# A fused six-part Macaron block on one NeuronCore: the last chunk's layer norm and choice of experts of the scan stage are made inside the second experts' stage

## The reference, cut to what matters

```python
x = L0_attn_x                                   # (8, 256, 256) float32
x = x + 0.5 * experts(layernorm(x))             # part 1, 16 experts, top 6, plus a shared one
x = x + selective_scan_block(layernorm(x))      # part 2, inner width 512, 16 states
x = x + 0.5 * experts(layernorm(x))             # part 3, the same weights as part 1
x = x + 0.5 * hadamard_ffn(layernorm(x))        # part 4
x = x + attention(layernorm(x))                 # part 5, 16 heads
x = x + 0.5 * hadamard_ffn(layernorm(x))        # part 6

def experts(x):
    scores = softmax(x @ gate_w.T)              # 16 experts
    w, ids = top_k(scores, 6); w = w / w.sum()
    c = combine(w, ids)                         # (token, expert) weights, 0 if not chosen
    out = sum_e c[:, e] * ((silu(x @ w1_e.T) * (x @ w3_e.T)) @ w2_e.T)
    return out + shared(x)
```

## Time and profile before

| | us |
|---|---|
| runs of the kernel | 2080.87, 2075.30, 2070.96 |
| median | 2075.3 |
| profiled execution, its time | 2073.7 |
| profiled execution, its span | 2071.9 |
| mean granted TensorE clock | 0.955 |

### The profile page before, as it was taken

The page is one execution under the profiler, slowest core; times in us unless marked ns, Lnnn a source line. Parts: engine busy times, 40 slices in busy tenths (PEclk is TensorE's granted clock), DMA queues, the critical chain, the costliest instruction groups (busy, mean ns, idle before and its releaser), DMA issues.

```text
span 2071.9 us, 26257 instructions
## 1 busy us (share of the span) xinstructions
PE 1865.6 (90%) x9448; PEld 1413.0 (68%) x9448; DVE 1353.3 (65%) x1828; ACT 933.4 (45%) x1769; POOL 570.6 (28%) x386
## 2 busy tenths in 40 slices
PE   5699999998779797898876999999999987999898
PEld 2488888887334353444434888888888875777787
DVE  4656656567099999989994565665676454666433
ACT  1223333333466577667552233332333326888322
POOL 1500000002177677677860000000000023555000
PEclk9899999999889999999997999999999988999999
DMA  4253223210022121122213232332221006653000
GB/s 175 88 155 103 77 86 103 62 62 26 21 66 76 57 66 62 56 66 62 69 53 92 85 104 62 100 95 71 62 74 50 1 8 140 113 115 73 31 21 21
DMA packets 86891, 150.86 MB, mean 73 GB/s; under 512 B 14376, under 2 KB 24232, under 8 KB 86248
## 3 DMA queue, kind: packets, MB, share of 16 engines
q1 hardware_dynamic: 86760, 149.17, 25.2%
HBM read 134.84 MB, written 14.29 MB: 72 GB/s over the span
## 4 chain that ended last, share of the span: by engine, by line
PE 72%; DVE 14%; issue 6%; ACT 5%; POOL 1%; SPq 1%; DMA 1%; DVEq 0%; ACTq 0%; POOLq 0%
PE psum L159 19%; PE psum L160 18%; PE psum L161 18%; DVE scan_state L1372 6%; PE psum L1225 4%; PE psum L1138 3%; PE psum L1165 1%; PE psum L1718 1%; DVE scan_state L1379 1%; PE psum L1146 1%; ACT attn_p L1850 1%; PE psum L1197 1%; PE psum L276 1%; PE psum L1697 1%; POOL scan_taps L1028 1%
## 5 line engine op out<-in xcount | busy, mean ns | idle before, releaser
L1041 POOL TENSOR_TENSOR scan_state<-scan_delta_u,scan_B_rows 128x1024 f32<-128x1024 f32 x128 | 301.8, 2367 | 171.5 <-PE psum L1225 124.0
L159 PE MATMUL psum<-xnT_hi,moe_w_hi 128*128 128x512 f32 x800 | 317.0, 396 | 4.6 <-DVE moe_w_lo L700 4.6
L160 PE MATMUL psum<-xnT_lo,moe_w_hi 128*128 128x512 f32 x800 | 315.5, 394 | 0.0
L161 PE MATMUL psum<-xnT_hi,moe_w_lo 128*128 128x512 f32 x800 | 312.9, 391 | 0.0
L1372 DVE TENSOR_TENSOR_SCAN scan_state<-psum,scan_state 128x1024 f32<-128x1024 f32 x128 | 292.2, 2283 | 3.1 <-POOL scan_state L1041 2.5
L768 DVE TENSOR_TENSOR moe_gated_up<-moe_gate_rows,psum 128x512 f32<-128x512 f32 x200 | 137.5, 688 | 239.2 <-PE psum L161 154.8
L410 POOL TENSOR_SCALAR rstd<-mean_var 128x2 f32<-128x2 f32 x48 | 10.7, 222 | 1020.0 <-DVE mean_var L444 1019.4
L724 ACT ACTIVATE moe_hidden<-psum 128x512 f32<-128x512 f32 x200 | 119.9, 600 | 377.4 <-PE psum L161 377.4
L1225 PE MATMUL psum<-scan_state,ident 128*128 128x512 f32 x512 | 255.8, 624 | 0.0
L159 PE MATMUL psum<-moe_w_hi,moe_hidden_hi 128*128 128x256 f32 x800 | 227.0, 284 | 9.1 <-DVE moe_hidden_lo L789 8.0
L161 PE MATMUL psum<-moe_w_hi,moe_hidden_lo 128*128 128x256 f32 x800 | 226.9, 284 | 0.0
(11 more groups left out here) (214 smaller groups left out, 3531.5 us busy)
## 6 DMA issues: line engine op xcount, KB each, us to landing
scan_B_rows<-scan_B SPq DMA_DIRECT2D x128, 256.0 KB, 3.1
moe_gate_rows<-gate_table SPq DMA_DIRECT2D x176, 128.0 KB, 2.9
moe_w_raw<-moe_pack SPq DMA_DIRECT2D x50, 384.0 KB, 3.8
attn_stack<-attn_rows SPq DMA_DIRECT2D x96, 128.0 KB, 5.4
moe_gate_rows<-gate_table SPq DMA_DIRECT2D x32, 224.0 KB, 3.0
ffn_w_raw<-ffn_pack SPq DMA_DIRECT2D x16, 384.0 KB, 3.7
moe_gate_rows<-gate_table SPq DMA_DIRECT2D x32, 160.0 KB, 2.7
moe_gate_rows<-gate_table SPq DMA_DIRECT2D x24, 192.0 KB, 2.9
```

Source lines behind the costliest of these rows:

```text
L159: e.matmul(out, wH, xH, start=start, stop=False)
L160: e.matmul(out, wH, xL, start=False, stop=False)
L161: return e.matmul(out, wL, xH, start=False, stop=stop)
L1041: e.tensor_tensor(self.st[q % self.NBUF][:], self.dtu[:, 2 * h:2 * h + 2, :], self.Bs[:, q % self.RING, :].unsqueeze(1).broadcast_to([P, 2 ...
```

## The change

For the experts' stage of part 3 a flag `guest` is set.

- `Tail.by_act` becomes a number: chunk 3 of the scan's tail normalises on DVE, with the shorter POOL sequence; chunks 0 to 2 stay on ACT.
- Jobs `g2` and `g3` of chunk 3 go from r = 23 and 25 to r = 4 and 5 (`LAST`). SP fetches the raw expert weights at r = 12 of chunk 3, ahead of that unit's B row, once g3's product is done. ACT splits the first tile at r = 24 (`lead_act`), DVE at r = 26 (`lead_dve`).
- PE runs gu(0) between the last y and out0. `tail.final` is left out on every engine.
- The tail of chunk 3 hangs behind steps 1 to 9 of the experts' stage: statistics at j = 1, 2, normalising at 2, 3, transposes at 2, 3, `xH` at 3, 4, `xL` at 4, `logits` at 5, `keep_logits` and `turn_logits` at 6, `choose` at 7, `turn_gates` at 8, `gates_hi` at 9. POOL runs its two steps from the experts' stage.
- SP stores the gates of chunks 0 to 2 right after the scan's last B row, waits for out1, fetches all five first gate rows, and stores chunk 3's gates at step 10, ahead of the gate rows of step 15.
- ACT waits for out1 before it splits the second tile.

```diff
-        if slot in (0, 2) and self.by_act:
+        if slot in (0, 2) and c < self.by_act:
...
-        if g == 0 and c == 0 and self.handed:
-            return self.before, NCH - 1, t
+        if (g == 0 and c == 0 and self.handed) or (self.guest and j < 10):
+            return self.before, NCH - 1, j
...
-    PE_SLOTS = {2: 1, 3: 3}
-    ACT_SLOTS = {3: 1, 4: 3}
+    PE_SLOTS = {2: 1, 3: 3, 5: 4, 6: 5, 8: 6}
+    ACT_SLOTS = {3: 1, 4: 3, 6: 4, 7: 5, 9: 6}
...
     def sync(self, e, meanwhile=None):
-        if self.prev:
+        if self.guest:
+            self.before.store_gates(e, self.gates[0], range(NCH - 1))
+            self.clear(e)
+            for j in range(self.PIECES):
+                self.piece(e, j)
+        elif self.prev:
             self.clear(e)
             self.first(e)
...
+                if self.guest and j + self.PIECES == self.G * (NCH - 1):
+                    self.before.store_gates(e, self.gates[0], (NCH - 1,))
...
+    def lead_pe(self, e):
+        self.gu(e, 0)
+
     def tensor(self, e):
-        self.gu(e, 0)
+        if not self.guest:
+            self.gu(e, 0)
...
     def lead_act(self, e):
-        self.prev.freed(e)
+        if self.guest:
+            self.prev.spent(e)
+        else:
+            self.prev.freed(e)
         self.split_hi(e, 0)
...
     def scalar(self, e):
         if not self.handed:
-            self.before.ready(e, NCH - 1)
+            if self.guest:
+                self.prev.freed(e)
+            else:
+                self.before.ready(e, NCH - 1)
...
+            if tt == 7 and self.guest:
+                tail.choose(e, tc, tail.bank())
...
+    LAST = {4: ("g2", 0), 5: ("g3", 0), 23: (None, 0), 25: (None, 0)}
...
+    def spent(self, e):
+
+        e.wait_ge(self.s_gin.sem, self.s_gin.at(4 * NCH))
+        e.wait_ge(self.s_Du.sem, self.s_Du.at(2 * NCH - 1))
+        e.wait_ge(self.s_dtu.sem, self.s_dtu.at(2 * NCH - 1))
...
     def sync(self, e):
         for q in range(self.N):
             c, h, n = self.unit(q)
+            if q == self.N - self.UNITS + 12 and self.next:
+                e.wait_ge(self.s_gin.sem, self.s_gin.at(4 * NCH))
+                self.next.first(e)
...
+        if self.next:
+            self.next.lead_pe(e)
         for name in ("out0", "out1"):
             job((name, NCH - 1), self.BANK)
-        self.tail.final(self.tail.pe, e)
+        if not self.next:
+            self.tail.final(self.tail.pe, e)
...
+            if q == self.N - 8 and self.next:
+                self.next.lead_act(e)
...
+            if q == self.N - 6 and self.next:
+                self.next.lead_dve(e)
```

More of the change, by code:

```diff
@@ L176, in __init__ @@
         self.home = None
-        self.by_act = False
+        self.by_act = 0
         self.back = back and not entry
@@ L386, in choose, with store_gates @@
         assert n[0] == self.r_v.per, n[0]
-    def store_gates(self, e, table):
-        for c in range(NCH):
+    def store_gates(self, e, table, chunks=range(NCH)):
+        for c in chunks:
             cols = slice(c * CHUNK, (c + 1) * CHUNK)
@@ L446, in norm @@
     def norm(self, e, c, p):
-        if self.last or self.by_act:
+        if self.last or c < self.by_act:
             return
@@ L500, in __init__ @@
         self.prev = self.next = None
-        self.handed, self.hands = handed, False
+        self.handed, self.hands, self.guest = handed, False, False
         tail.spare = True
@@ L595, in sync @@
     def sync(self, e, meanwhile=None):
-        if self.prev:
+        if self.guest:
[4 more added lines that the diff above has]
+        elif self.prev:
             self.clear(e)
             self.first(e)
-        if self.gates:
+        if self.gates and not self.guest:
             for j in range(2):
@@ L604, in sync @@
                 self.piece(e, j)
+        if self.gates:
             for j in range(self.N):
@@ L619, in pool @@
     def pool(self, e):
-        if self.handed:
+        if self.handed or self.guest:
             for slot in (0, 2):
@@ L673, in tensor @@
             tail, c, t = self.behind(j)
-            if t in self.PE_SLOTS:
+            if t in self.PE_SLOTS and (t < 5 or self.guest):
                 tail.pe(e, c, self.PE_SLOTS[t])
@@ L729, in scalar @@
             tail, c, t = self.behind(j)
-            if t in self.ACT_SLOTS:
+            if t in self.ACT_SLOTS and (t < 5 or self.guest):
                 tail.act(e, c, self.ACT_SLOTS[t])
@@ L916, in __init__ @@
         self.s_o = Sem(k, "o")
-        tail.by_act, tail.s_pw = True, Sem(k, "pw", 4, passes=NCH)
+        tail.by_act, tail.s_pw = NCH - 1, Sem(k, "pw", 4, passes=NCH)
         self.prior, used = {}, {}
@@ L983, in job @@
         name, ahead = self.JOBS.get(r, (None, 0))
+        if c == NCH - 1:
+            name, ahead = self.LAST.get(r, (name, ahead))
         return (name, c + ahead) if name and 0 <= c + ahead < NCH else None
@@ L1060, in pool @@
                 self.tail.pool(e, c - 1, 0 if r == 7 else 2)
-        for slot in (0, 2):
-            self.tail.pool(e, NCH - 1, slot)
+        if not self.next:
+            for slot in (0, 2):
+                self.tail.pool(e, NCH - 1, slot)
     def normed(self, e, c, i):
@@ L1357, in scalar @@
                 rows_hi(c + 1)
-        self.tail.final(self.tail.act, e, self.next and self.next.lead_act)
+            if q == self.N - 8 and self.next:
+                self.next.lead_act(e)
+        if not self.next:
+            self.tail.final(self.tail.act, e)
     def vector(self, e):
@@ L1428, in vector @@
             add(NCH - 1, p)
-        self.tail.final(self.tail.dve, e, self.next and self.next.lead_dve)
+        if not self.next:
+            self.tail.final(self.tail.dve, e)
 class Attention:
@@ L2111, in program @@
                                  (gates, ins["ones"]), tails[n - 1], tails[n]))
+                if n == 3:
+                    parts[-1].guest = tails[n - 1].spare = True
                 if n == 1:
```

5 lines of the change are left out of this document (3 added, 2 removed).

## The result

The changed kernel took 2063.7 us (median of 8 runs, 2058.3 to 2070.6) against 2078.1 for the kernel before (8 runs): ratio 0.9934, 95% interval 0.9917 to 0.9950. In a second series it took 2067.5 (7 runs) against 2075.6 (12 runs): 0.9952, 0.9932 to 0.9973. The forecast was 2062, with 2056 to 2071 as its range. The profiled execution took 2066.6 us. Two medians that say 14.4 and 8.2 us call for a finer measure. I took one from the traces: the time from the first recurrence (r = 0) of chunk 3 to the first split of the stage behind the second experts. It holds all that the change touches. It was 571.7 us before and 561.0 after, **10.7 us less**; 10.7 of the second series' 2075.6 would be a ratio of 0.9948. The prediction gave 0.56 to a gain beyond 0.5%: the result lies on that line, with 0.9934 on one side of it, 0.9952 just on the other, and both intervals reaching 0.9950.

What follows compares the result with a forecast made beforehand. DVE was taken to pace the scan, PE the experts' steps, with a chain between them. gu(2) 15.7 us earlier, less 3.9 us of PE work in the steps, gave -11.8 from 2073.7: 2061.9 us, range 2056 to 2071.

Steps and rivals of the forecast that it cites:

- late decays at r = 8, 9: Scan chunk 3: gate jobs at r = 4 and 5 make ACT deliver decays(8) and decays(9) late; +1.9 us.
- split at r = 26: Scan chunk 3: DVE's split_lo of the first tile, 0.95 us alone, overlaps its neighbour by 0.1; +0.9 us.
- gu(0) ahead of out0: End of the scan: PE's 2.75 us for gu(0) fall half into the wait for scan_gated; +1.3 us.
- out1's end to gu(2): Seam into the experts' stage: gu(2) starts 8.1 us after out1's end, bounds 7.3 and 10.6.
- PE's work in the steps: Experts' steps: transposes, logits and turns in PE's queue count in full; +3.9 us, bounds 2.0 and 7.5.
- The fall of the clock: Seam: PE's 1.9 us pause before gu(1) would lower its clock, ending gu(1) near 6.1 instead of 4.7; free.
- rivals 1 and 3: Experts' steps: 0 to 9 DVE-bound, 2070.7 us, chance 0.16; PE's five slots wait for their links, 2076.2, chance 0.04.
- rival 2: Scan stage: gate job wholly on the path (+1.4), POOL starved for a B row (+2.5); 2065.8 us, chance 0.09.
- The raw loads: Scan chunk 3, r = 12: five loads ahead of the B row cost nothing, with 2.5 us of cover.
- Rival 4: ACT's gate jobs: each table switch costs double, lateness grows by 5.2 us; 2067.1 us, chance 0.02.
- Rival 5: Seam: gu(2) not brought forward, only the scan's +2.8 and gu(0)'s +1.3 are left; 2077.8 us, chance 0.03.
- the terms named for the lower end, 2056: Whole kernel: no late decays, the lower ends of 8.1 (seam) and of 3.9 (steps).

Runs made afterwards that it cites:

- e8: Kernel before with only chunk 3's gate jobs g2 and g3 moved to r = 4 and 5; traced stretch 575.1 us against 571.7 before.
- e2: Changed kernel with gate job g3 at r = 6 in place of 5, g2 left at 4; traced stretch 559.7 us against 561.0.
- e3: Changed kernel with DVE's split of the first tile behind the last weighing in place of r = 26; traced stretch 560.0 us against 561.0.
- e1: Changed kernel with g2 and g3 at r = 6 and 8, raw loads left at r = 12; traced stretch 563.5 us against 561.0.
- e4: Changed kernel with DVE's split of the first tile at r = 30 in place of 26; traced stretch 559.9 us against 561.0.
- e6: Changed kernel with gate jobs and raw loads spaced, split later, low part earlier, ACT, DVE and SP released by the last scan_gated; 2058.1 us, 0.9912 of before.

## Why the prediction was right, point by point

| term | forecast | measured |
|---|---|---|
| late decays at r = 8, 9 | +1.9 | +1.84 |
| fall of PE's clock behind them | none | +1.70 |
| split at r = 26 | +0.9 | +2.14 |
| gu(0) ahead of out0 | +1.3 | +1.1 |
| PE's clock phase after r = 31 | none | -1.1 |
| out1's end to gu(2), 8.1 in place of 27.9 | -19.8 | -19.9 |
| PE's work in the steps | +3.9 | +3.5 |
| sum | -11.8 | -10.7 |

**The two large terms** were right, and they carry the result. Out1's end to gu(2) was forecast at 8.1 and took 8.0, with the late gate row as what ends last. The fall of the clock that the prediction expected behind PE's pause of 1.9 us did not come: gu(1) ran at 1.00 from 1115.90 to 1118.60. It had been priced at nothing, so the sum didn't feel it. In the steps PE's small products stand in its queue and are paid in full; the waits of PE from 1120 to 1540 us, kernel after, hold only that before down(0) (they answer to the earlier trace rows):

```profile
PE psum L159 <- DVE moe_hidden_lo L809: 1.6, 1, 1.6
```

So rivals 1 and 3 did not come about; in every run with the change gu(2) to the next stage is 413.4 to 414.0 us. The choice in step 7 caused two table loads on ACT that I had not counted:

```profile
1149.79 1.28 ACT L343 ACT_TABLE_LOAD   x1
1151.36 1.28 ACT L743 ACT_TABLE_LOAD   x1
```

They cost nothing: no wait of PE follows them.

**The late decays** were right to a tenth: 0.70 + 0.97 us of idle DVE, put down to ACT. **What hung on them was missed**: I looked at DVE's loss and not at what a pause of DVE does to PE, though the same text knew that a pause of 2.2 us goes with a clock of 0.50 and used it for gu(1). So rival 2 was right that the scan stage pays more, by 2.9 us before what the clock gave back, but by neither of its two ways. e8 shows the 1.70 by themselves, e2 shows them gone with one wait less.

**The split** was mis-sized: 0.95 us was read where POOL is idle. The trace of before has the warning, which I did not read: the subtractions for the next chunk's rows of B and C, like the split with two inputs in SBUF. The 10.17 us are shown above; the one behind r = 27 of chunk 2, timelines of DVE and POOL, kernel after:

```profile
954.04 2.44 DVE L1406 TENSOR_TENSOR scan_BC<-scan_weighted,scan_BC 32x512 fp32r<-32x512 f32 x1
```
```profile
953.54 2.39 POOL L1119 TENSOR_TENSOR scan_delta<-scan_delta,scan_log 128x1024 f32<-128x1024 f32 x1
```

2.44 us for 512 elements a partition, beside a product of POOL (2.44 also before, at 954.31). The Trainium skill (SBUF — State Buffer, SBUF: two separate sides) states that a DVE operation with two SBUF inputs and a GpSimd operation that reads SBUF hold one port pair in turn, and that whoever comes second waits for the whole instruction. By that rule the split would end 0.95 behind 1079.24, at 1080.2; it ended at 1080.06. The trace agrees to 0.1 us, and the term would have been 2.2. For the subtraction of 10.17 us one instruction's wait is not enough: it started 0.37 us before a product of POOL ended, and four more products went ahead of it.

**The clock phase after r = 31** paid 1.1 us back (16.69 where 16.66 + 1.1 was due). `scan_gated`, which needs the last y, starts 6.0 us after the recurrence of r = 31 in after, 7.1 in before and 7.0 in e3, as PE rose earlier to its full clock (0.73 from 1097.30 on, above, against 0.62 in e3 and in before). Window, kernel before:

```profile
1091.90:1098.90 7.00, 6.85 (x13) 2.98 (x13) 3.52 (x3) 0.59 (x1) 0.00 (x0) 0.62 0.00 0
```

It goes with the split: with gu(0) ahead of out0, r = 31 to out1's end is 16.7 to 16.9 us in every kernel that splits between two recurrences (after, e1, e2, e4), and 17.7 to 17.8 in the two that split behind the last weighing (e3, e6). So the split at r = 26 cost 2.14 and gave 1.1 back, 1.0 in all, near the forecast 0.9 by luck. How PE's pause there moves the later rise of its clock no run settles. In the sum, too, part of the agreement is luck: +1.7 and +1.2 missed on one side, -1.1, -0.2, -0.1 and -0.4 on the other.

**The raw loads** cost nothing, as forecast; e1 showed how near the other case lies. **Rival 4** is out by the kernel after as well. Timeline of ACT, a gate job of chunk 3:

```profile
998.05 1.28 ACT L1298 ACT_TABLE_LOAD   x1
999.35 0.60 ACT L1298 ACTIVATE scan_silu_gate<-psum 128x512 f32<-128x512 f32 x1
999.96 1.28 ACT L1299 ACT_TABLE_LOAD   x1
```

From one start to the next it is 1.30 us, with SiLU right behind the load. **Rival 5** is out: gu(2) came 14.2 us sooner in the stretch (forecast 15.7). Its sum leaves out the 3.9 us of the steps; with them it is 2081.7.

**The whole time.** 2061.9 was counted from one profiled execution, which had the subtraction of 10.17 us in it. The profiled execution of after, 2066.6, lies 4.7 above: 1.1 for the sum, the rest from stages that the change doesn't touch (+3.8, -6.5 and +6.2, see above). That the median of 2063.7 fell nearer is the luck of the series. The bounds have a slip as well: the terms named for the lower end, 2056, give 2061.9 - 1.9 - 0.8 - 1.9 = 2057.3.

## What to carry to other kernels

When an engine off the pace is made late for a unit or two, count three things: the pace setter's own loss, the pause that it hands to TensorE, and what TensorE delivers late once its granted clock has fallen. Price an operation that is moved by a row in which its new neighbours are at work, not by its best row; here the same trace had a subtraction at 10.17 us that takes 0.68 alone. And a product that is moved forward is worth its place only if the last input of what follows it comes early too: here a gate row, not gu(0), set the start of down(0).

## What the runs showed of the hardware

- A DVE subtraction with two SBUF inputs did next to nothing while POOL ran its products: 2.22 us in place of 0.95, with 1.40 beside POOL; a small one took 2.44 beside one product and 10.17 where POOL's products followed each other without a gap, 0.68 alone. The recurrences (2.28 to 2.29 us) and the weighing (1.22), each with an input in PSUM, kept their times beside POOL.
- PE waits of 2.04 and 2.31 us, 4.5 apart, went with a fall of the granted clock to 0.76, while one of 2.03 followed by one of 1.25 did not. A single one of 2.24, in e1 before 1002.95, was followed by 3.2 us at 0.50. 1.93 and 1.55 left it at 1.00 in down(0), 1.93 and 1.82 went with 0.55 in another execution of the same program. The length of the waits alone does not foretell it.
- Five loads of 384 KB ahead of a small one on SP's queue kept POOL 7.2 us waiting for it, though each issue takes only some 0.45 us (2.23 for five).
- Executions of one program differed by 4.0 us in the attention stage (180.8 and 184.8, with a granted clock of 0.80 and 0.71 over its first 40 us), by 6.7 us in chunk 1 of the scan (138.14 and 131.45, by one subtraction), and by 1.3 at the seam (1.0 of it with the clock).
